# Routing with one late table in place of two, single reads before SP's first row loads, and W1 copies moved to ScalarE

## The reference

```python
x = x + attention(layernorm(x))       # x: 4 batches x 512 tokens x 128
h = layernorm(x)                      # 2048 tokens
router_probs = softmax(h @ Wr)        # 8 experts
expert_idx = argmax(router_probs);  p_max = max(router_probs)
out_t = p_max * (gelu(h_t @ W1[e] + b1[e]) @ W2[e] + b2[e])   # e = expert_idx of the token
x = x + out                           # W1: 8 x 128 x 512, W2: 8 x 512 x 128
```

## Time and profile before

| what | value |
|---|---|
| median of 3 runs | 101.15 us (100.6 to 101.19) |
| profiled execution, its own time | 100.89 us |
| its span | 99.1 us |
| PE busy in the span | 88.6 us (89%) |
| DVE, ACT, POOL busy | 70.9, 57.3, 58.0 us |

### The profile page before, as it was taken

How to read it: one execution, slowest core, us unless ns; L and a number is a source line. 1 busy time by engine, 2 the same in 40 slices (tenths; PEclk the granted TensorE clock), 3 DMA queues, 4 the chain that set the end, 5 groups by cost and what they waited for, 6 DMA issues and landing times.

```text
span 99.1 us, 2603 instructions
## 1 busy us (share of the span) xinstructions
PE 88.6 (89%) x720; PEld 79.1 (80%) x721; DVE 70.9 (71%) x322; ACT 57.3 (58%) x179; POOL 58.0 (59%) x100
## 2 busy tenths in 40 slices
PE   3979999999989888999999999999999999999700
PEld 1337978979877777978789899999999999999600
DVE  5689975569779897977899959769567668644400
ACT  3245786666822615627387689766785776776300
POOL 6463837934076858776417708777766745754640
PEclk9999999999999999999999999999999999999995
DMA  0999999991000011114220314634611000100000
GB/s 21 348 309 380 386 305 292 315 310 39 0 27 27 27 41 51 39 43 105 62 61 27 109 43 120 162 106 120 150 45 53 16 10 10 34 26 23 0 0 0
DMA packets 12125, 10.52 MB, mean 106 GB/s; under 512 B 1472, under 2 KB 9920, under 8 KB 12112
## 3 DMA queue, kind: packets, MB, share of 16 engines
q1 hardware_dynamic: 10576, 7.82, 28.4%
q0 software_dynamic: 1248, 2.14, 6.5%
q10 hardware_dynamic: 288, 0.40, 1.1%
HBM read 7.68 MB, written 3.13 MB: 109 GB/s over the span
## 4 chain that ended last, share of the span: by engine, by line
PE 66%; DVE 15%; issue 3%; ACT 3%; DMA 3%; POOL 3%; POOLq 2%; DVEq 1%; ACTq 0%
PE psum L1335 20%; PE psum L1318 20%; PE psum L1119 4%; PE psum L1161 4%; DMA x_sb<-in_x_dram 3%; DVE sc L730 3%; PE psum L1196 3%; PE psum L1302 3%; DVE zed L726 2%; PE psum L1178 2%; PE psum L1187 2%; PE psum L1139 2%; POOLq L83 2%; DVE st L746 2%; POOL rs L394 1%
## 5 line engine op out<-in xcount | busy, mean ns | idle before, releaser
L425 POOL DMA_INDIRECT out_dram<-slot x23 | 24.0, 1044 | 14.9 <-DVE slot L993 9.6
L615 ACT ACTIVATE hid<-psum,b_sb 128x128 f32<-128x128 f32 x92 | 26.4, 371 | 8.3 <-PE psum L1318 8.3
L1318 PE MATMUL psum<-tT,w_st 128*128 128x128 f32 x184 | 24.6, 276 | 0.3 <-ACT tT L606 0.2
L1335 PE MATMUL psum<-w_sb,hid 128*128 x184 | 24.5, 277 | 0.0
L1318 PEld LDWEIGHTS psum<-tT,w_st 128*128 128x128 f32 x184 | 22.4, 192 | 0.7 <-ACT tT L606 0.7
L1335 PEld LDWEIGHTS psum<-w_sb,hid 128*128 128x128 f32 x184 | 22.3, 192 | 0.4
L417 POOL DMA_INDIRECT routed_rows<-rows,slot_at x16 | 16.3, 1017 | 10.6 <-issue 3.4
L993 DVE SCALAR_TENSOR_TENSOR slot<-psum,slot 128x128 f32<-128x128 f32 x23 | 8.0, 347 | 9.2 <-PE psum L1335 9.1
L1246 PE MATMUL psum<-ones_bf 128*128 128x256 bf16 (+1 forms) x59 | 10.6, 331 | 1.6 <-DVE ones_bf L648 1.5
L957 DVE COPY w_st<-w_sb 128x512 f32 x17 | 7.7, 456 | 3.2 <-PE psum L1318 2.0
L1246 PEld LDWEIGHTS psum<-ones_bf 128*128 128x128 bf16 x60 | 6.2, 105 | 4.4 <-issue 2.4
(11 more groups left out here) (203 smaller groups left out, 151.2 us busy)
## 6 DMA issues: line engine op xcount, KB each, us to landing
w_sb<-in_W_dram SPq DMA_DIRECT2D x2, 1024.0 KB, 8.4
w_sb<-in_W_dram SPq DMA_DIRECT2D x4, 512.0 KB, 9.7
slot<-routed_rows SPq DMA_DIRECT2D x23, 66.0 KB, 2.0
x_sb<-in_x_dram SPq DMA_DIRECT2D x3, 256.0 KB, 4.6
routed_rows<-pad_rows SPq DMA_DIRECT2D x1, 528.0 KB, 5.6
b_sb<-in_b_dram SPq DMA_DIRECT2D x1, 512.0 KB, 6.7
out_dram<-slot POOLq DMA_INDIRECT x23
w_sb<-in_wcat_dram ACTq DMA_DIRECT2D x1, 264.5 KB, 3.4
```

Of the source, the lines that this page charges most:

```text
L425: pool.indirect_dma_start(out=out_flat, out_offset=bass.IndirectOffsetOnAxis(ap=slot[:, i, NUMBER:NUMBER + 1].bitcast(U32), axis=0), in_=s ...
L615: act.activation(hid[:, i % 2, c, :], src[:, c * P:(c + 1) * P], ACT.Gelu, bias=b1_sb[:, bass.ds(expert[i] * FC + c, 1)]).then_inc(hid_s, 1)
L1318: last = pe.matmul(dst[:, c * P:(c + 1) * P], w1_st[:, i % W1_RING, c * P:(c + 1) * P], tT[:, i % RING, :], start=True, stop=True)
L1335: last = pe.matmul(y_ps[i % 2][:, 0:D], hid[:, i % 2, c, :], w2_sb[c][:].rearrange("p e d -> p (e d)")[:, bass.ds(expert[i] * D, D)], star ...
```

## The change

One chain makes the late table. The small tables `start_c` and `expert_c` and their chain are gone, and tiles 5 and 6 read the first two columns of `start_b` and `expert_b`. SP reads the start of each of tiles 0 to 4 by itself, just ahead of that tile's load, where it read all five at once. ACT copies the W1 blocks of tiles 0 to 7 (before: 0, 1, 2, 5, 6, 7), and DVE begins with tile 8. ACT reads one expert number, copies block 0, reads two more, copies block 1, and copies block 2 behind `normal_rows(1)`; `copy_tT(1)` comes ahead of the tanh of the last batch's logits. The numbers of the fourth and fifth group of `keep_warm` go from 22 and 2 to 15 and 4.

```diff
--- before.py
+++ after.py
@@ -30,7 +30,7 @@
 LN_EPS = 1e-5
 DEN_EPS = 1e-6
 WARM_START = (10, 2)
-WARM_LAST = (2, 18, 4, 22, 2)
+WARM_LAST = (2, 18, 4, 15, 4)
 
 
 def preln_linear_attention_moe(nc, x, wcat, bias, W1, b1, W2, b2, out):
@@ -56,7 +56,7 @@
     W1_RING = EARLY
     HB_ACT = 2
     W1_ACT = 3
-    W1_BY_ACT = (0, 1, 2, EARLY, EARLY + 1, EARLY + 2)
+    W1_BY_ACT = EARLY + MIDDLE + 1
     PACK_SHIFT = 13
     PACK = 1 << PACK_SHIFT
     P_SHIFT = 7
@@ -181,12 +181,6 @@
         step_own = sb("step_own", [P, len(BEHIND) * E - 1])
         step_last = sb("step_last", [P, len(BEHIND) * E - 1])
         step_b = sb("step_b", [P, 1, len(BEHIND) * E - 1])
-        past_c = sb("past_c", [P, MIDDLE, len(BEHIND) * E - 1])
-        stepped_c = sb("stepped_c", [P, MIDDLE, len(BEHIND) * E - 1])
-        stepped_cn = sb("stepped_cn", [P, MIDDLE])
-        packed_c = sb("packed_c", [P, MIDDLE], I32)
-        start_c = sb("start_c", [P, MIDDLE], I32)
-        expert_c = sb("expert_c", [P, MIDDLE], I32)
...
@@ -295,7 +289,7 @@
         def late_values(engine, i):
             g = i - EARLY
             if g == 0:
-                return tile_values(engine, expert_c, E - 1)
+                return tile_values(engine, expert_b, E - 1, slice(0, MIDDLE))
             return tile_values(engine, expert_b, E - 1, slice(g, min(g + GROUP, LATE)))
 
         def late_group(i):
@@ -331,24 +325,23 @@
                         sp.wait_ge(rows_out[b][g], 16 * (end - begin))
 
             sp.wait_ge(early_start, 1)
-            at = tile_values(mybir.EngineType.SP, start_a, (E + 1) * REGION - P)
             for b in range(B - 2):
                 sp.wait_ge(rows_out[b][0], 16 * J)
             for i in range(EARLY):
+                at = tile_values(mybir.EngineType.SP, start_a, (E + 1) * REGION - P, slice(i, i + 1))
                 rows_there(B - 2, AHEAD, i)
-                sp.dma_start(slot[:, i, :], rows_dram[bass.ds(at[i], P), :]).then_inc(slot_in[i], 16)
+                sp.dma_start(slot[:, i, :], rows_dram[bass.ds(at[0], P), :]).then_inc(slot_in[i], 16)
 
 
             def load(i, at):
                 rows_there(B - 1, BEHIND, i)
                 sp.dma_start(slot[:, i, :], rows_dram[bass.ds(at, P), :]).then_inc(slot_in[i], 16)
 
-            sp.wait_ge(middle_start, 1)
-            at = tile_values(mybir.EngineType.SP, start_c, (E + 1) * REGION - P)
+            sp.wait_ge(late_start, 1)
+            at = tile_values(mybir.EngineType.SP, start_b, (E + 1) * REGION - P, slice(0, MIDDLE))
             for i in range(MIDDLE):
                 load(EARLY + i, at[i])
 
-            sp.wait_ge(late_start, 1)
             sp.wait_ge(pads_out, 16)
             ends = list(range(MIDDLE, LATE, GROUP)) + [LATE]
             for low, high in zip(ends, ends[1:]):
@@ -591,10 +584,11 @@
             act.preload_act_table(ACT.Gelu)
             copy_scT(B - 1)
             act.wait_ge(early_expert, 1)
-            expert = list(tile_values(mybir.EngineType.Activation, expert_a, E - 1, slice(0, W1_ACT)))
+            expert = list(tile_values(mybir.EngineType.Activation, expert_a, E - 1, slice(0, 1)))
             act.wait_ge(w1_in, 32)
-            for i in range(W1_ACT):
-                stage_w1(i)
+            stage_w1(0)
+            expert += tile_values(mybir.EngineType.Activation, expert_a, E - 1, slice(1, W1_ACT))
+            stage_w1(1)
 
             def normal_rows(i):
                 act.wait_ge(slot_in[i], 16)
@@ -619,9 +613,10 @@
             normal_rows(0)
             copy_tT(0)
             normal_rows(1)
+            stage_w1(2)
+            copy_tT(1)
             act.wait_ge(lms_s, B - 1)
             act.activation(ex[:, tiles(B - 1), :], lms[:, tiles(B - 1), :], ACT.Tanh, scale=0.5).then_inc(ex_s, 1)
-            copy_tT(1)
             gelu(0)
             expert += tile_values(mybir.EngineType.Activation, expert_a, E - 1, slice(W1_ACT, EARLY))
             for i in range(SLOT_TILES):
@@ -629,8 +624,10 @@
                     copy_tT(i + 2)
                 if i + 1 < SLOT_TILES:
                     gelu(i + 1)
+                if i + W1_ACT < EARLY:
+                    stage_w1(i + W1_ACT)
                 if i == 2:
-                    act.wait_ge(middle_expert, 1)
+                    act.wait_ge(late_expert, 1)
                     expert += late_values(mybir.EngineType.Activation, EARLY)
                     stage_w1(EARLY)
                 if i == 3:
@@ -964,9 +961,6 @@
                 dve.tensor_scalar(hb[:, i % H_RING, :], slot[:, i, xs], slot[:, i, SCALE:SCALE + 1],
                                   slot[:, i, SHIFTED:SHIFTED + 1], ALU.mult, ALU.add).then_inc(h_s, 1)
 
-            dve.wait_ge(w1_in, 32)
-            for i in range(W1_ACT, EARLY):
-                stage_w1(i)
             residual(B - 1)
             moments2(B - 1)
             route(B - 1)
@@ -1017,55 +1011,41 @@
             late(6)
             late_step(dve.scalar_tensor_tensor(out=step_last[:], in0=step_last[:], scalar=float(P),
                                                in1=packed_steps[:, 0:SB - 1], op0=ALU.mult, op1=ALU.add))
-            late_step(dve.tensor_tensor(past_c[:], tile_no[:, 0:MIDDLE, 0:SB - 1],
-                                        incl_b[:, 0:SB - 1].unsqueeze(1).broadcast_to([P, MIDDLE, SB - 1]), ALU.is_ge))
+            late_step(dve.tensor_tensor(past_b[:], tile_no[:, :, 0:SB - 1],
+                                        incl_b[:, 0:SB - 1].unsqueeze(1).broadcast_to([P, LATE, SB - 1]), ALU.is_ge))
             late(8)
             late_step(dve.scalar_tensor_tensor(out=step_b[:, 0, :], in0=step_own[:], scalar=float(PACK - P),
                                                in1=step_last[:], op0=ALU.mult, op1=ALU.add))
             normal_rows(HB_ACT + 1)
             late(10)
-            late_step(dve.tensor_tensor(stepped_c[:], past_c[:], step_b[:].broadcast_to([P, MIDDLE, SB - 1]), ALU.mult))
+            late_step(dve.tensor_tensor(stepped_b[:], past_b[:], step_b[:].broadcast_to([P, LATE, SB - 1]), ALU.mult))
+            output_rows(0, biased=False)
             late(11)
-            late_step(dve.tensor_reduce(stepped_cn[:], stepped_c[:], AX_X, ALU.add))
+            late_step(dve.tensor_reduce(stepped_n[:], stepped_b[:], AX_X, ALU.add))
             late(12)
-            late_step(dve.scalar_tensor_tensor(out=packed_c[:], in0=stepped_cn[:], scalar=first_base[:],
-                                               in1=packed_row0[:, 0:MIDDLE], op0=ALU.add, op1=ALU.add))
-            late(13)
-            dve.tensor_scalar(start_c[:], packed_c[:], PACK_SHIFT, P_SHIFT, ALU.logical_shift_right,
-                              ALU.logical_shift_left).then_inc(middle_start, 1)
-            dve.tensor_scalar(expert_c[:], packed_c[:], PACK_SHIFT + REGION_SHIFT - P_SHIFT, E - 1,
-                              ALU.logical_shift_right, ALU.bitwise_and).then_inc(middle_expert, 1)
-            output_rows(0, biased=False)
-            late_step(dve.tensor_tensor(past_b[:], tile_no[:, :, 0:SB - 1],
-                                        incl_b[:, 0:SB - 1].unsqueeze(1).broadcast_to([P, LATE, SB - 1]), ALU.is_ge))
-            late(14)
-            late_step(dve.tensor_tensor(stepped_b[:], past_b[:], step_b[:].broadcast_to([P, LATE, SB - 1]), ALU.mult))
-            normal_rows(HB_ACT + 2)
-            late(15)
-            late_step(dve.tensor_reduce(stepped_n[:], stepped_b[:], AX_X, ALU.add))
-            output_rows(1, biased=False)
-            late(16)
             late_step(dve.scalar_tensor_tensor(out=packed_b[:], in0=stepped_n[:], scalar=first_base[:],
                                                in1=packed_row0[:], op0=ALU.add, op1=ALU.add))
-            late(17)
+            late(13)
             late_step(dve.tensor_scalar(short_b[:], packed_b[:], PACK - 1, None, ALU.bitwise_and))
             late_step(dve.tensor_scalar(own_b[:], packed_b[:], PACK_SHIFT, P_SHIFT, ALU.logical_shift_right,
                                         ALU.logical_shift_left))
-            late(18)
+            late(14)
             late_step(dve.tensor_scalar(again[:], short_b[:], -float(PACK // 2), 0.0, ALU.add, ALU.min))
-            late(20)
+            late(16)
             dve.tensor_tensor(start_b[:], own_b[:], again[:], ALU.add).then_inc(late_start, 1)
             dve.tensor_scalar(expert_b[:], packed_b[:], PACK_SHIFT + REGION_SHIFT - P_SHIFT, E - 1,
                               ALU.logical_shift_right, ALU.bitwise_and).then_inc(late_expert, 1)
+            normal_rows(HB_ACT + 2)
+            output_rows(1, biased=False)
             normal_rows(EARLY)
             output_rows(2, biased=False)
             late_step(dve.tensor_scalar(skip_row[:], again[:], part_no[:], float(-SKIP), ALU.add, ALU.mult))
-            dve.wait_ge(middle_expert, 1)
+            dve.wait_ge(late_expert, 1)
             expert += late_values(mybir.EngineType.DVE, EARLY)
             dve.wait_ge(late_expert, 1)
```

(16 more changed lines are left out.)

## The result

| | before | after |
|---|---|---|
| median of 20 runs each | 100.83 us (100.6 to 101.6) | 101.31 us (100.97 to 101.84) |
| ratio | | 1.0044 (95%: 1.0026 to 1.0063) |
| profiled execution's span | 99.1 us | 99.6 us |

The change makes the kernel 0.44% slower, 0.44 us. The 20 runs of the kernel before have a lower median than the three that the prediction had.

What follows compares the result with a forecast made beforehand. PE bounds the kernel, busy 89% of the span, almost alone from 49.94. The sum of +0.57 us gave 101.46 from the profiled execution and 101.72 from the median; the middle, 101.6, was forecast, range 100.6 to 102.5.

Steps and rivals of the forecast that it cites:

- `hidden(1)`: PE's matmuls before the late tiles: start at about 49.55, not 49.94, 0.4 us gained, 0.3 to 0.55 with the bounds.
- the sum: Delay of tile 7's transpose on PE: 0.87 - d + 0.25 = 1.12 - d, +0.57 us with d = 0.55.
- the refill's 0.25: Behind a hole, PE's transpose and next `down` cost more, 0.30 + 1.08 against 0.11 + 1.02: 0.25 us for tile 5.
- d: How much earlier DVE's late-table chain starts: 0.55 us as read, 0.8 if nothing holds DVE, 0.1 if tile 2 lands late.
- A: Experiments' theory: one late table makes tiles 5 and 6 wait, 1.1 us with no head start, swallowing the front's gain.
- The single reads on SP: SP reading one tile start ahead of each load: 0.39 us per read, 0.35 to 0.5 kept as bounds.
- the late chain: DVE's wide instructions making the late table: starts at 51.76 - d, table written at 54.84 - d.
- The holes: PE's idle time: ahead of tile 4's transpose growing from 0.13 to 0.35 us, a new 0.5 ahead of tile 5's.
- rival 3: ACT becomes the bound: copies of 0.65 and a register read make five tiles run at 1.95, +0.3, 102.0; chance 0.04.
- rival 4: PE's clock falls for a stretch through the thinner warm-up: +1 to +2 us, 102.8; chance 0.03.
- rival 2: SP's single reads cost as much as two or more, DVE hangs on tile 2: +1.0 to +1.2, 102.3; chance 0.11.
- Rival 1: Gain kept: wide chain some 0.3 shorter, hole ahead of tile 5's transpose shrinks, -0.3 us, 100.8; chance 0.14.

## Why the prediction was right

Two rows of the trace before, `hidden(1)` and T5, that the first points go back to:

```profile
49.94 1.16 PE L1318 MATMUL psum<-tT,w_st 128*128 128x128 f32 x8 [0.20 <-ACT tT L606]
...
57.13 0.27 PE L1302 MATMUL psum<-ident,hb 128*128 128x128 f32 x1
```

- **Sign and size.** +0.57 us forecast as the sum, +0.44 measured. The time, 101.31, lies in the range; my 101.6 stood on a median of three that was 0.3 high. That the sum came so near is in part luck, as the next points show.
- **The sum counted 0.16 twice.** I took T5's delay from 57.13, where it was issued before the change, and the refill's 0.25 from the chain, which counts T5 from 57.29. Counted from 57.13, T5 and the next `down` took PE 1.28 before and take 1.38 now, so the refill adds only 0.10. On one count the sum is 0.96 - d, +0.41 with my d, and not 1.12 - d. T7 came 0.47 late in the trace. For the late table alone the one count gives about +1.0, not A's +1.1; +1.3 was measured.
- **The mechanism.** T5 held by its load, whose start comes from the late table: forecast 57.45, found 57.50. Table written near 54.3, found 54.37. Tile 5's load forecast at 55.05, found at 55.04. The refill behind the hole, 0.30 + 1.08, is there to the digit. The run with the late table alone and the run with the small one put back show that it is the table.
- **Three terms were mis-sized.** The single reads on SP: 0.28 for all but the first, not 0.39, and 0.47 for the first. Tile 0's load came near my 44.41 all the same, at 44.33; the offset of the traces is 0.09 of that. `hidden(1)`: 49.17, not 49.55. I took its old start less 0.4; but before, PE had stood 0.20 for the transposed copy of tile 1, which was now done at 48.82, so PE went from `hidden(0)` through the rank sums into `hidden(1)` without a stop. The head start d: 0.79 between the traces, its upper bound, not 0.55, because tile 2's load landed in 2.2 and not 2.3 after an issue 0.3 earlier than forecast.
- **One term was missing.** I laid out the late chain at 2.9 with tile 3's rows filling a gap. In fact the rows waited 0.23 for their load (3.19 us to land, 1.8 in the trace before), and the chain from `past_b` to `start_b` took 3.22, 0.31 more than the same chain took where that load was in time. This took back what the larger d gave, and the table came where I had put it. With d = 0.79 and no such wait the sum, on one count, would have been +0.17; with the wait it is +0.48, against 0.47 in the trace. The same wait added 0.5 in the trace of the table alone. I had the row of that wait in view (tile 3's load waits for batch 2's last scatter) and said that it cost nothing that PE sees; it does, through DVE's order.
- **The holes came out the other way round.** Forecast: 0.35 ahead of T4 and a bigger one, 0.5, ahead of T5. Found: 0.51 ahead of T4, since the table came 0.08 late and the rows behind it took 0.53 and not 0.40; and as T4 was late itself, 0.35 ahead of T5 by the forecast's count (T4 + 2.11, the step of before), of which the trace has PE idle for 0.19. T3's 0.16 wasn't forecast; the bigger wait swallowed it.
- **The rivals.** ACT was never the bound (rival 3), the granted clock stayed at 1.00 from 45 to 53 us in windows of one microsecond (rival 4), and of SP's reads only the first cost what a read of two does, so tile 2's load wasn't held up (rival 2). Rival 1, the gain kept, needed the big table 0.3 sooner; the small table put back keeps 0.3 us of it. (Six instructions of the small table are gone from DVE, not the five named above.)
- **The Trainium skill** ("DMA: Bandwidth & Descriptors", Latency and other measured facts) gives a floor of about 600 ns for such a read. The trace doesn't agree: 0.47 for SP's first read of one value and 0.27 to 0.28 for the other four, and tile 2's load went at 46.03, not at the 47.0 that the page would give.

## What to carry to other kernels

Where a table has several consumers and the first of them stands at the end of read, load and landing, ask what the first one pays before the small table made for it is merged into the big one. Here it paid for the width of instructions that it didn't need: about 0.75 us, with a front that had gained nearly as much. When a chain of small steps decides, look at each instruction between them that waits for something else, above all for a DMA; one late load holds the whole chain. And if a chip has holes of its own, look where they lie before a ratio from it is believed.

## What the runs showed that I had not expected

- A register read on SP costs 0.47 for one value where it is the first behind the table's semaphore, 0.27 to 0.28 for each that follows, 0.48 for two and 0.75 for five, but 0.87 to 1.00 for four from the late table; on ACT 0.48 to 0.49 for one and mostly 0.5 for two (0.62 once), but 1.0 for three. Its price isn't a line in the number of values, and why the first costs more is open.
- Tile 3's load, always issued just as the last scatter of batch 2 has landed, took 1.8 us in the trace before and 3.0, 3.2 and 3.7 in three traces of other kernels without holes, one of which changes nothing on SP ahead of it. On chips 12 and 13 two traces have 1.8 and 1.9. What makes it slow is open.
- The same program takes 101 us on some chips and 112 to 117 on others, with PE's granted clock at 0.98 to 1.00 and mostly 0.92 to 0.98. The two traces of the changed kernel differ by 12.5 us in span, and in the longer one ACT stands for 11.6 in a handful of stalls whose releaser is not in the trace, the first, 4.38, right behind its table load. From 45 to 60 us the granted clock is 0.77 there.
